# Attention with a mixture of experts on one core: value products grouped by four, two, two and four, and the maxima split in PSUM

## The reference

```
qkv = x @ W_qkv                  # 256 x 768; 16 heads of 16
q, k = rope(q), rope(k)
w = softmax(causal(q @ k.T / 4)) # per head, 1024 x 1024
x = layernorm(x + (w @ v) @ W_o)
g = softmax(x @ Wg + bg)         # 8 experts, the best two kept and renormalized
out = layernorm(x + sum_e g_e * (x @ We[e].T + be[e]))
```

## Time and profile before

| | |
|---|---|
| median of three runs | 3255.22 us |
| profiled execution | 3256.74 us |
| its span (first to last instruction) | 3255.0 us |
| TensorE busy | 3120.2 us, 96% |
| VectorE busy | 2690.9 us, 83% |
| ScalarE busy | 1886.4 us, 58% |
| GpSimd busy | 1212.6 us, 37% |
| granted TensorE clock, mean | 0.977 |

### The profile page before, as it was taken

One profiled execution on the slowest core, in us unless ns is written; L12 is line 12 of the kernel. 1 busy time (PEld: TensorE's weight loads), 2 busy tenths in 40 slices (PEclk: granted clock), 3 DMA queues, 4 the chain that ended last, 5 costly groups with the idle time before them and its releaser, 6 DMA issues. The chain is left out here.

```text
span 3255.0 us, 58560 instructions
## 1 busy us (share of the span) xinstructions
PE 3120.2 (96%) x18752; PEld 1714.3 (53%) x18752; DVE 2690.9 (83%) x8448; ACT 1886.4 (58%) x4257; POOL 1212.6 (37%) x1418
## 2 busy tenths in 40 slices
PE   5789999999999999999999999999999999999987
PEld 2234555555555555565555555555555555555555
DVE  5877888989888888888988888888888888898745
ACT  2266556565565656556575655656565565755651
POOL 4153424343243443424344342434334244432110
PEclk7699999999999999999999999999999999999997
DMA  6444324333442434334333442433443243334000
GB/s 135 66 65 81 60 59 74 64 70 66 78 64 48 79 59 76 60 78 64 53 73 61 82 65 60 71 64 68 66 82 60 59 75 62 70 64 68 2 27 13
DMA packets 174819, 210.95 MB, mean 65 GB/s; under 512 B 26008, under 2 KB 124592, under 8 KB 174256
## 3 DMA queue, kind: packets, MB, share of 16 engines
q1 hardware_dynamic: 173056, 202.98, 35.5%
q10 hardware_dynamic: 1456, 4.23, 0.3%
HBM read 138.44 MB, written 67.11 MB: 63 GB/s over the span
## 5 line engine op out<-in xcount | busy, mean ns | idle before, releaser
L645 ACT ACTIVATE weights<-scores 128x512 f32<-128x512 f32 (+3 forms) x3072 | 1334.0, 494 | 904.8 <-PE scores L979 891.7
L772 DVE CUSTOM_DVE_ANT_0 bank<-bank,far_q 128x128 f32<-128x128 f32 (+3 forms) x2048 | 963.3, 512 | 204.4 <-PE bank L963 188.5
L963 PE MATMUL bank<-k_stack,q_stack 96*128 96x512 bf16 (+3 forms) x3072 | 808.8, 334 | 47.0 <-DVE z L872 11.2
L979 PE MATMUL scores<-q_stack,k_stack 99*128 99x512 bf16 (+3 forms) x3072 | 822.7, 329 | 10.8 <-ACT weights L645 7.3
L562 POOL TENSOR_SCALAR_AFFINE_SELECT weights<-weights 128x512 f32<-128x512 f32 x512 | 326.2, 639 | 1260.2 <-ACT weights L645 1259.9
L775 DVE TENSOR_REDUCE maxima<-bank 128x1 f32<-128x512 f32 x1024 | 643.6, 681 | 70.8 <-PE bank L963 70.5
L1001 PE MATMUL attend<-weights,values 128*32 128x512 f32 (+3 forms) x6144 | 581.5, 494 | 1.0 <-POOL weights L562 0.9
L963 PEld LDWEIGHTS bank<-k_stack,q_stack 96*128 96x128 bf16 x3072 | 277.9, 98 | 422.5 <-issue 155.1
L979 PEld LDWEIGHTS scores<-q_stack,k_stack 99*128 99x128 bf16 x3072 | 280.8, 98 | 412.0 <-ACT weights L645 153.4
L906 PE MATMUL bank<-wexp_hi,zT_hi 128*128 128x512 f32 x1024 | 380.7, 453 | 1.6
L880 DVE SCALAR_TENSOR_TENSOR z<-bank,picked,z 128x256 f32<-128x256 f32 x512 | 247.1, 483 | 113.8 <-PE bank L906 106.1
(11 more groups left out here) (109 smaller groups left out, 3169.4 us busy)
## 6 DMA issues: line engine op xcount, KB each, us to landing
parts_scratch<-parts SPq DMA_DIRECT2D x128, 384.0 KB, 2.5
q_stack<-parts_scratch SPq DMA_DIRECT2D x384, 128.0 KB, 7.1
k_stack<-parts_scratch SPq DMA_DIRECT2D x384, 128.0 KB, 7.7
x_in<-in_x SPq DMA_DIRECT2D x64, 256.0 KB, 2.9
z<-in_x SPq DMA_DIRECT2D x32, 512.0 KB, 5.3
out<-z SPq DMA_DIRECT2D x32, 512.0 KB, 2.9
q_stack<-lowrows SPq DMA_DIRECT2D x192, 8.0 KB, 2.0
z<-in_w_exp ACTq DMA_DIRECT2D x1, 1024.0 KB, 14.1
```

The source lines that it names most:

```text
L645: act.activation(weights[:, n % NW, hh, c0:CH], st[(QUAD * n + hh) % NS][:, c0:CH], ACT.Exp, scale=DH ** -0.5).then_inc(S["weights_ready"], 1)
L772: dve.tensor_tensor_reduce(out=b[:, 0:w], in0=b[:, 0:w], in1=far_q[:, CH - w:CH], scale=1.0, scalar=-SENTINEL, op0=ALU.add, op1=ALU.max, a ...
L963: pe.matmul(b[:, 0:w], q_stack[0:ROWS, n, hh, qt * P:(qt + 1) * P], k_stack[0:ROWS, n, hh, kc * CH:kc * CH + w], start=True, stop=True).th ...
L979: pe.matmul(st[(QUAD * n + hh) % NS][:, c0:CH], k_stack[0:MROWS, s, hh, kb * P:(kb + 1) * P], q_stack[0:MROWS, s, hh, qc * CH + c0:(qc + 1 ...
```

## The change

- The buffer weights is handed out by columns: three blocks of the same size as before, and an item that is narrow shares a block. weights_at gives the place, BEFORE how many items back the value product lies for which the first exponential of an item waits.
- In ORDER the value products are put so that a slot's twelve items come as 4, 2, 2 and 4; in places other steps stand inside a group. The last four of a batch (LATE) are done in the next pass. All steps are the same, 608 words; their order is new.
- MT keeps what is left of the maxima in the bank, beside the maxima, instead of in SBUF, and releases the bank with its last operation. SyncE waits for that release; the semaphore maxrows_ready goes.
- SyncE no longer waits at the end of a batch for the store; XR waits for the store of the same half of z instead.

```diff
-NW = 3
+BLOCK = 4 * CH
+BEFORE = (4, 4, 4, 0, 4, 4, 3, 3, 3, 3, 3, 5)
+LATE = 4
+def weights_at(batch, n):
+    s, it = divmod(n, ITEMS)
+    step = (0, 1, 2, 2, 0, 1, 2, 0, 1, 2, 0, 2)[it]
+    return (SLOTS * batch + s + step) % 3 * BLOCK + (3 * CH if it in (3, 11) else 0)
...
+XL.0 XL.1 XT.0 XL.2 XT.1
+ST.0.0 ST.0.1 B.0.0.0 B.0.0.1 MC.3 B.0.0.2 ST.0.2 PV.44 PV.45 PV.46 XL.3 PV.47 YE.3.1 B.0.0.3 B.0.1.0 B.0.1.1
+  ST.0.3 VCOPY.3 MASK.0 XR.0 XR.1 XT.2 B.0.1.2
...
+ST.4.0 ST.4.1 B.0.3.3 LOAD.0 ST.4.2 PV.0 PV.1 PV.2 PV.3 B.0.4.0 YE.0.0 ST.4.3 B.0.4.1 QK.0.0 ROPE.0.0
...
+ST.11.0 N1A.1 GLT.0 B.0.11.0 ST.11.1 QK.0.3 ST.11.2 ST.11.3 GA.0 B.0.11.1 B.0.11.2 GB.0 B.0.11.3 MASK.11
+ST.12.0 ST.12.1 ST.12.2 B.1.0.0 PV.8 PV.9 PV.10 GT.0 B.1.0.1 B.1.0.2 MC.0 PV.11 B.1.0.3 YE.0.1 ST.12.3 B.1.1.0
+  B.1.1.1 MASK.12
...
+ST.24.0 ST.24.1 B.2.0.0 B.2.0.1 B.2.0.2 ST.24.2 MC.1 PV.20 ROPE.1.0 B.2.0.3 B.2.1.0 B.2.1.1 B.2.1.2 PV.21 PV.22
+  PV.23 YE.1.1 ST.24.3 MASK.24 B.2.1.3 LOAD.2 B.2.2.0 B.2.2.1
...
+ST.46.0 ST.46.1 B.3.10.2 B.3.10.3 ST.46.2 ST.46.3 B.3.11.0 B.3.11.1 MASK.46
+ST.47.0 ST.47.1 VP.3 ST.47.2 B.3.11.2 B.3.11.3 ST.47.3 MASK.47
...
@@ MT on VectorE
-                    dve.tensor_tensor(maxrow_err[:, :], src, maxrow[:, 0], ALU.subtract).then_inc(fr, 1)
-                    emptied(dve, c, step)
-                    link(c, step, dve.tensor_copy(maxrow[:, 1], maxrow_err[:, :]))
-                    dve.tensor_tensor(maxrow[:, 2], maxrow_err[:, :], maxrow[:, 1], ALU.subtract) \
-                        .then_inc(S["maxrows_ready"], 1)
+                    link(c, step, dve.tensor_tensor(rest_of, src, maxrow[:, 0], ALU.subtract))
+                    link(c, step, dve.tensor_copy(maxrow[:, 1], rest_of))
+                    dve.tensor_tensor(maxrow[:, 2], rest_of, maxrow[:, 1], ALU.subtract).then_inc(fr, 1)
...
@@ the exponential, on ScalarE
-                        if n >= NW:
-                            act.wait_ge(S["attended"], c.at("attended", ("PV", n - NW)))
+                        before = n - BEFORE[n % ITEMS]
+                        if before < 0 and c.seg not in ("pre", "first"):
+                            done(act, c, "attended", ("PV", before + SLOTS * ITEMS))
+                        elif 0 <= before < n:
+                            done(act, c, "attended", ("PV", before))
...
@@ SyncE
-                elif kind == "END" and ("stored", c.seg) in BOOK:
-                    sp.wait_ge(S["stored"], c.at("stored", ("N2A", 1), DMA))
+                    if c.seg != "mid" or c.turn > 0:
+                        sp.wait_ge(S[f"stored{g}"], c.from_start(f"stored{g}", 0, DMA))
```

More of the change, by code:

```diff
@@ L100 @@
[L100 to L106, removed]
@@ L133 @@
[L133 to L138, removed]
@@ L256, in ledger @@
                 add("link", seg, step)
+            if step[0] == "N2A":
+                add(f"stored{step[1]}", seg, step)
             if step[0] == "XR":
@@ L311, in so_far, with earlier, latest @@
         return self.from_start(name, n, per)
-    def prev(self, name, step, per=1):
-        before = SEGMENTS[:SEGMENTS.index(self.seg)]
-        offsets = []
-        for order in (before, before + ("mid",)) if self.seg == "mid" else (before,):
-            back = 0
-            for seg in reversed(order):
-                steps = BOOK.get((name, seg), ())
-                if step in steps:
-                    offsets.append(-back - steps[::-1].index(step))
-                    break
-                back += len(steps)
-        assert offsets and len(set(offsets)) == 1, (self.seg, name, step, offsets)
-        return self.from_start(name, offsets[0], per)
+def earlier(c):
+    if c.seg == "mid":
+        return Count("mid", c.turn - 1) if c.turn else Count("first")
+    return {"first": lambda: Count("pre"), "last": lambda: Count("mid", NMID - 1), "post": lambda: Count("last")}[c.seg]()
+def latest(c, step):
+    while step not in plan(c.seg):
+        c = earlier(c)
+    return c
 def attention_moe_kernel(nc, x, w_qkv, w_o, w_gate, b_gate, w_exp, b_exp, rot_cos, rot_sin, out):
@@ L416, in projected @@
         def projected(eng, c):
-            before = {"first": ("pre",), "last": ("mid", NMID - 1)}.get(c.seg)
-            if c.seg == "mid":
-                before = ("mid", c.turn - 1) if c.turn else ("first",)
-            emptied(eng, Count(*before), ("VP", TILES // 2 - 1))
+            emptied(eng, c, ("VP", TILES // 2 - 1), prev=c.seg != "pre")
         def filled(eng, c, step):
@@ L428, in emptied, with done, item_weights @@
         def emptied(eng, c, step, prev=False):
+            c = latest(earlier(c) if prev else c, step)
             b = bank(c.seg, step)
-            eng.wait_ge(free[b], (c.prev if prev else c.at)(f"bank{b}", step))
+            eng.wait_ge(free[b], c.at(f"bank{b}", step))
+        def done(eng, c, name, step):
+            eng.wait_ge(S[name], latest(c, step).at(name, step))
+        def item_weights(batch, n):
+            kb, qc = ITEM[n % ITEMS]
+            w = CH - score_width(kb, qc)
+            place = weights_at(batch, n)
+            return weights[:, place:place + QUAD * w].rearrange("p (j c) -> p j c", j=QUAD)
         def run(eng, work):
@@ L521, in work @@
                     sp.wait_ge(S["normed"], c.at("normed", step))
-                    sp.dma_start(out_d[batch - 1, :, 4 * g:4 * g + 4, :], z[:, g]).then_inc(S["stored"], DMA)
-                elif kind == "END" and ("stored", c.seg) in BOOK:
-                    sp.wait_ge(S["stored"], c.at("stored", ("N2A", 1), DMA))
-                    sp.sem_inc(S["sp_waits"], 1)
+                    sp.dma_start(out_d[batch - 1, :, 4 * g:4 * g + 4, :], z[:, g]).then_inc(S[f"stored{g}"], DMA)
+                elif kind == "END" and c.seg == "post":
+                    wait_all(*((f"stored{g}", c.at(f"stored{g}", ("N2A", g), DMA)) for g in range(2)))
             run(sp, work)
```

148 lines of the change are left out of this document (73 added, 75 removed).

## The result

The changed kernel takes 3264.42 us (median of 7 runs, 3260.18 to 3266.51) against 3255.22 (3251.53 to 3257.09) for the kernel before on the same chip: ratio 1.0028, interval [1.0018, 1.0037]. It is 9 us slower where 28 us of gain were forecast. The answer, ahead of the evidence: the longer groups gave their 15 us and the new order cost 32 us in waits; the split in PSUM is worth 8.5 us in the old order and nothing in the new one, where the collision that it mends no longer happens. From the kernel before that makes -8.5 - 15 + 32, about 9.

A forecast was written before the change was run, and what follows sets the result against it. TensorE was taken as the bound, busy 190.72 of 192.50 us a batch. From 3256.74, groups (15.1) and split (13.5) leave 3228.1; 1.5 less to match the median gives 3226.6, say 3227, range 3215 to 3238.

The forecast's parts named there:

- The groups: Value products on TensorE: each group costs 0.24 us whatever it holds; 63 groups fewer gain 15.1 us.
- The maxima split in PSUM: MT on VectorE: no more 1.09 us a batch lost beside GpSimd's rotation product; 0.9 over 15 batches, 13.5 us gained.
- The buffer and SyncE: Weights' buffer waits, paid by ScalarE's 75 us of slack, and SyncE's dropped wait for the store: both priced 0.
- the margin at ST.x.3: Scores behind a group of four: the needed exponential is done at 1.75 us, TensorE arrives at 2.5; margin 0.7, priced 0.
- The boundary: Batch end, XT.0 and XT.1 waiting for banks: 0.9 us both before and after the change, so 0.
- The rest of the order: All other steps, same but permuted: 0 taken; 2 us a batch less or 4 us more held possible.
- the third: Rival: waits of the new order, 1.9 us a batch, give everything back; 3255, within 0.2%; 13 in 100.
- The fourth: Rival: slower, TensorE stands at ST.x.3 for late exponentials behind long groups; at 0.35 us a place 3269; 12 in 100.
- The first rival: Both gains hold but the new order waits 0.9 us a batch more elsewhere, ahead of GT.0: 3240; 16 in 100.

The follow-up runs named there:

- e8: Old order with new buffer and PSUM split, 20 pairs of value products cut apart (45 groups a batch for 25): 3315.52 us, ratio 1.0184 to the kernel before.
- e3: The changed kernel with MT's split back in SBUF, everything else as changed: 3263.38 us, ratio 1.0029 to the kernel before.
- e14: Old order with new buffer, PSUM split and banks turned by two at MOE.1.1.0, plus MT.0 moved ahead of B.1.2.0: 3233.55 us, ratio 0.9936.
- e2: The changed kernel with ORDER as before and LATE 2 for 4; new buffer, PSUM split and SyncE change kept: 3246.45 us, ratio 0.9971.
- e1: The kernel before with only MT's maxima split moved to PSUM; order, buffer and SyncE as before: 3246.47 us, ratio 0.9973.
- e13: The changed kernel with banks turned by two at MOE.1.3.3, plus GT.1, GLT.0, WO.0.0 and B.0.8.0 moved one to four steps later: 3262.02 us, ratio 1.0026.

## Why the prediction was wrong

By its own steps:

- **The groups: 15.1 us.** Right. The price is per group, 0.23 when groups are added (e8); four items of one group take 2.29 where 2.28 was forecast; the two orders differ by 16.3 us once VectorE and ScalarE are relieved.
- **The maxima split in PSUM: 13.5 us.** The mechanism is right (1394 to 279 ns), the term is mis-sized and, for this kernel, counted in the wrong place. It was read from the old order and added to the new: there MT.0 no longer meets the rotation, and the split is worth nothing (e3). In the old order it is worth 8.5, because the bank's later release was priced at 0 for the places of the new order; at the old place it costs 0.74 of TensorE's time a batch. With that wait taken away (e14) the gain over the kernel before is 21 us, some 17 without the turned banks, above the 13.5; a part of it may be the moved step's own. What the forecast should have asked: is the collision of the earlier trace rows still there in the order for which it is counted?
- **The buffer and SyncE: 0.** Right for the old order (e2 and e1 differ by 0.02 us). For the new one the margin at ST.x.3 held, but "ScalarE stands idle meanwhile, which its 75 us pay" was let go at no price. The idle time is 209 us in 104 times, 16 us a batch, and the exponentials behind it have to be caught up; how much of the 32 us below comes from it no run shows.
- **The boundary: 0.** Wrong by its size. It was to cost 0.9 before and after; after, it costs 1.25 (0.99 for XT.0 and 0.26 for XT.1), and without it the kernel is 11 us faster. The reduction that XT.0 waits for starts 0.56 behind its product (1450.30 to 1450.86), as forecast, but XT.0 starts 0.91 behind that and not 0.70: the read of the accumulator behind the reduction (0.14) and the start behind the release were left out. XT.1 then waits for the second reduction (1451.48) in the same way.
- **The rest of the order: 0 taken.** This is the step that failed. With the boundary in it, it costs 18.0 + 14.5 = 32.5 us against the old order (63 x 0.23 = 14.5 for the groups), 2.0 us in each middle batch by the lost time (10.26 - 8.30). It stood inside the bounds given (2 less to 4 more), at their other side; "the same steps permuted" isn't "the same waits". I had priced the gathered products as a saving alone, and not as the loss of the cover that they give where they stood. "VectorE and ScalarE have 27 and 75 us of slack" was read as cover everywhere; it is an average over 192 us, and the waits are of 0.2 to 1.0 us at twenty places in which the engine has two or three operations to do at once.

Of the rivals, the third is nearest: all given back by waits of the order at 1.9 us a batch. Its time didn't come: 3264 lies outside its 0.2% around 3255, and on the slower side, to which only the fourth had given a chance. It had 13 in 100 and no mechanism, only a sum. The fourth, which was to hold the slower side, didn't occur: the wait of the scores' weight loads for exponentials fell to 89.4 us in 272 times, from this row of the kernel before, 335.94 to 2838 us:

```profile
PEld scores L979 <- ACT weights L645: 106.8, 296, 0.8
```

Slower came by many small waits that I had not made one case. The first rival named GT, and there it was partly right: GT.1 costs 0.41 and GLT.0 0.24 a batch, GT.0 nothing.

What stays open: which of the twenty small places a better new order would mend. One edit that moved four of them made it worse (e13), so the 34 us of lateness are shown as a sum and for two places (XT.0 and ST.45.3), not one by one. Open too is how much of it is lost cover and how much ScalarE's idle time behind the long groups: no run gives the buffer a fourth block.

## What to carry to other kernels

Before gathering work of the bound engine into longer groups, ask what it covers where it stands: work that needs nobody is the time in which others catch up, and here 0.23 us saved a group was paid with 0.5 us of waits. Ask also what the gathered work holds back: a buffer's place that comes free later stops the engine that fills it. Read a gain from the order in which it will be used: a collision or a bank's release found in the old order may not exist in the new one. And when an order is rewritten, forecast it by the distance from each producer's start to its consumer at the places where the other engines have several operations in a row, not by their share of busy time.

## What the runs showed of the hardware

- A VectorE copy of 8 columns with input and output in SBUF took 1.19 us and a cast of 32 columns 1.17, beside GpSimd products of 1.16 us that ran at the same time; otherwise 165 and 182 ns. Both have one input. The prediction took the collision's price from the subtraction with two inputs in SBUF alone; its own row of a cast with one input at 687 ns shows that two inputs aren't needed. The Trainium skill (SBUF: State Buffer, "Who interferes with whom") lists copy and cast among the operations that can enter a mode with both SBUF ports and so can contend with GpSimd; that these two contend, the rows here show. With its input in PSUM a cast of 128 columns stayed at 268 to 280 ns in 104 cases. In e1 30 of the 64 second casts, whose input lies in PSUM, start while a GpSimd product is running, and the longest of all takes 279 ns.
- A relieved engine can slow a kernel: exponentials cut to 128 columns cost 30 us in one order, since they moved other work into such a collision. Behind its stall of 2 us TensorE's granted clock fell to 1.2 GHz for 3.4 us in 6 of 14 batches; behind the 1.0 us at XT.0 in the changed kernel it never did.
- A subtraction that writes to PSUM and reads PSUM and SBUF took 287 ns, 8 more than the one that writes to SBUF.
